# Cross-attention with an FP4 feed-forward: the group loop written out, the FP4 chain for h and the down product moved

## The reference

```python
x = x + tanh(g_xattn[0]) * xattn(layernorm(x), ctx, Wq, Wk, Wv, Wo, bo)
x = x + tanh(g_ffn[0]) * ffn(layernorm(x), w_gate, w_up, w_down)
# xattn: softmax(q k^T / 8) v per head, then @ Wo + bo
# ffn:   h = silu(fp4(x) @ fp4(w_gate).T) * (fp4(x) @ fp4(w_up).T); fp4(h) @ fp4(w_down).T
# fp4:   per 16 values: scale = max(|v|)/6; v/scale to the nearest of 0, .5, 1, 1.5, 2, 3, 4, 6; times scale
```

## Time and profile before

| | us |
|---|---|
| median of 3 runs | 598.71 (597.97 to 600.03) |
| the profiled execution | 598.33 |
| its span, first to last instruction | 596.1 |
| busy: PE, DVE, ACT, POOL | 543.8, 476.7, 312.3, 276.3 |

### The profile page before, as it was taken

One profiled execution on the slowest core, in us unless ns is written; L12 is line 12 of the kernel. 1 busy time (PEld: TensorE's weight loads), 2 busy tenths in 40 slices (PEclk: granted clock), 3 DMA queues, 4 the chain that ended last, 5 costly groups with the idle time before them and its releaser, 6 DMA issues.

```text
span 596.1 us, 9833 instructions
## 1 busy us (share of the span) xinstructions
PE 543.8 (91%) x2841; PEld 335.7 (56%) x2841; DVE 476.7 (80%) x793; ACT 312.3 (52%) x723; POOL 276.3 (46%) x234
## 2 busy tenths in 40 slices
PE   5889999999999998999999998999999999999642
PEld 4655565666566554666466554665566565656331
DVE  2769875889977996889977995789977997787655
ACT  3434756575456645575456644566456745546211
POOL 4007344553828173553828173363827264456400
PEclk9779999999999999999999999999999999999675
DMA  8500000200020000200020000200020000000000
GB/s 158 99 1 1 1 1 0 52 2 1 1 58 2 0 2 9 50 0 0 1 56 1 0 0 9 50 0 0 1 56 1 0 0 5 1 1 1 1 3 3
DMA packets 27892, 9.31 MB, mean 16 GB/s; under 512 B 24016, under 2 KB 27600, under 8 KB 27856
## 3 DMA queue, kind: packets, MB, share of 16 engines
q1 hardware_dynamic: 27856, 8.92, 7.5%
HBM read 8.50 MB, written 0.41 MB: 15 GB/s over the span
## 4 chain that ended last, share of the span: by engine, by line
PE 59%; DVE 27%; issue 10%; ACT 2%; DMA 1%; DVEq 0%; POOL 0%; SPq 0%; POOLq 0%; ACTq 0%
PE attn L789 16%; PE scores L775 11%; PE ring L728 10%; DVE max L897 8%; PE scores L776 7%; PE ring L735 4%; PE ring L742 4%; DVE f_abs L362 3%; DVE f_abs L364 2%; DVE e_gate L860 2%; DVE acc_v L919 2%; PE ring L707 2%; DVE h_fp L366 1%; DVE z L871 1%; DVE rsum L904 1%
## 5 line engine op out<-in xcount | busy, mean ns | idle before, releaser
L634 ACT ACTIVATE probs<-scores 120x400 f32<-120x400 f32 (+1 forms) x384 | 190.0, 504 | 211.7 <-PE scores L776 209.1
L897 DVE TENSOR_REDUCE max<-ring 116x1 f32<-116x482 f32 (+1 forms) x336 | 204.7, 649 | 28.4 <-PE ring L728 24.1
L505 POOL TENSOR_TENSOR acc_p<-acc_p,probs 120x800 f32<-120x800 f32 x79 | 156.3, 1978 | 61.7 <-ACT probs L634 58.1
L789 PE MATMUL attn<-probs,ctx_n 120*64 120x400 f32 (+1 forms) x768 | 173.9, 532 | 0.0
L775 PE MATMUL scores<-q_hh,k_hl 128*120 128x400 f32 (+1 forms) x384 | 155.0, 404 | 1.2 <-DVE q_ls L899 1.2
L775 PEld LDWEIGHTS scores<-q_hh,k_hl 128*120 128x120 f32 (+1 forms) x384 | 70.9, 185 | 128.2 <-ACT probs L634 70.2
L776 PE MATMUL scores<-q_ls,k_h 71*120 71x400 f32 (+1 forms) x384 | 134.8, 351 | 0.0
L728 PE MATMUL ring<-k_hl,q_hh 128*116 128x482 f32 (+1 forms) x336 | 119.6, 409 | 12.4 <-DVE max L897 4.7
L776 PEld LDWEIGHTS scores<-q_ls,k_h 71*120 71x120 f32 (+1 forms) x384 | 71.6, 186 | 4.2
L728 PEld LDWEIGHTS ring<-k_hl,q_hh 128*116 128x116 f32 (+1 forms) x336 | 59.1, 182 | 25.7 <-DVE max L897 9.9
L789 PEld LDWEIGHTS attn<-probs,ctx_n 120*64 120x64 f32 (+1 forms) x768 | 38.3, 136 | 46.4 <-issue 34.3
(11 more groups left out here) (127 smaller groups left out, 526.9 us busy)
## 6 DMA issues: line engine op xcount, KB each, us to landing
ctx_n<-in_ctx SPq DMA_DIRECT2D x16, 360.0 KB
wq<-in_L_xattn_Wq SPq DMA_DIRECT2D x1, 512.0 KB, 4.6
wo<-in_L_xattn_Wo SPq DMA_DIRECT2D x1, 512.0 KB, 6.8
x_in<-in_x SPq DMA_DIRECT2D x8, 50.0 KB
out<-y_out SPq DMA_DIRECT2D x8, 50.0 KB
wk<-in_L_xattn_Wk SPq DMA_DIRECT2D x1, 256.0 KB, 4.1
ctx_n<-in_ctx SPq DMA_DIRECT2D x16, 1.0 KB
wv<-in_L_xattn_Wv SPq DMA_DIRECT2D x1, 256.0 KB, 6.3
```

The source lines that it names most:

```text
L505: pool.tensor_tensor(acc_p[0:r, t.g % 2, :], left, probs[0:r, c % PROBS, :], ALU.add).then_inc(sum_p, 1)
L634: act.activation(probs[0:r, c % PROBS, k * HALF:(k + 1) * HALF], scores[0:r, slot % SCORE_BANKS, 0:HALF], ACT.Exp).then_inc(probs_full, 1)
L789: mm = pe.matmul(attn[64 * i:64 * i + C, k, 0:HALF], ctx_n[0:r, par, c, 0, :], probs[0:r, c % PROBS, k * HALF:(k + 1) * HALF], start=(j == ...
L897: dve.tensor_reduce(max3[0:rows, tile, part:part + 1], src[0:rows, 0:MAXC[part + 1] - MAXC[part]], AX.X, ALU.max).then_inc(free, 1)
```

## The change

The loop is gone: all 16 groups are written out on every engine, and the waits hold constants. In groups 3, 5, ..., 13 the nine links for h stand at slots 18 to 23, behind the maxima, and the transposes of h_fp4 and the down product stand in the even group after it, at slots 2, 3 and 5; its store follows there. Group 15 keeps the old slots (LAST_H_SLOTS, LAST_FFN_SLOTS), and the finish is as before.

```diff
-FFN_SLOTS = {2: ('zT', 0), 4: ('gate', 0), 6: ('up', 0), 19: ('hT', 0), 20: ('hT', 1), 22: ('down', 0)}
-W_SLOTS = {slot: ("wT", i) for i, slot in enumerate(FFN_SLOTS)}
+FFN_SLOTS = {2: ('zT', 0), 4: ('gate', 0), 6: ('up', 0)}
+DOWN_SLOTS = {2: ('hT', 0), 3: ('hT', 1), 5: ('down', 0)}
+LAST_FFN_SLOTS = {**FFN_SLOTS, 19: ('hT', 0), 20: ('hT', 1), 22: ('down', 0)}
+W_SLOTS = {slot: ("wT", i) for i, slot in enumerate(LAST_FFN_SLOTS)}
...
-H_SLOTS = [7, 8, 9, 10, 11, 12, 13, 14, 16]
+H_SLOTS = [18, 19, 19, 20, 21, 21, 22, 22, 23]
+LAST_H_SLOTS = [7, 8, 9, 10, 11, 12, 13, 14, 16]
...
-    if g % 2 and slot in FFN_SLOTS:
-        keys += [(FFN_SLOTS if g >= 3 else W_SLOTS)[slot]]
+    ffn = W_SLOTS if g == 1 else LAST_FFN_SLOTS if g == GROUPS - 1 else FFN_SLOTS if g % 2 else DOWN_SLOTS if g >= 4 else {}
+    if slot in ffn:
+        keys += [ffn[slot]]
...
+    def down_batch(self):
+
+        return self.batch(-1 if self.g % 2 or self.g == GROUPS else -2)
...
-            for g in (0, 1):
-                group(Turn(g))
-            with engine.Fori(0, (GROUPS - 4) // 4) as p:
-                for g in (2, 3, 4, 5):
-                    group(Turn(g, p))
-            for g in (GROUPS - 2, GROUPS - 1):
+            for g in range(GROUPS):
                 group(Turn(g))
             finish(Turn(GROUPS))
...
-                b, par = t.batch(-1), t.parity(-1)
+                b = t.down_batch()
+                par = b % 2
...
-                if t.g % 2 and t.g >= 3:
+                if t.g % 2 == 0 and t.g >= 4 or t.g == GROUPS - 1:
                     store(t)
...
-                    pe.wait_ge(hq4, LINKS * t.batch())
+                    pe.wait_ge(hq4, LINKS * (t.down_batch() + 1))
...
-                        if slot in H_SLOTS:
-                            h_fp4_link(t, H_SLOTS.index(slot))
+                        slots = LAST_H_SLOTS if t.g == GROUPS - 1 else H_SLOTS
+                        for link in [i for i in range(LINKS) if slots[i] == slot]:
+                            h_fp4_link(t, link)
```

More of the change, by code:

```diff
@@ L129, with __init__ @@
 RING = number_ring()
[L130 to L136, removed]
 class Turn:
-    def __init__(self, g, p=0):
-        self.g, self.p = g, p
+    def __init__(self, g):
+        self.g = g
     def count(self, per_group, plus):
-        return per_group * self.g + plus + (4 * per_group) * self.p
+        return per_group * self.g + plus
     def batch(self, ahead=0):
-        return self.g // 2 + ahead + 2 * self.p
+        return self.g // 2 + ahead
     def parity(self, ahead=0):
@@ L156, in fills @@
     def fills(self, ahead=0):
-        return (self.g // 2 + ahead) // 2 + 1 + self.p
+        return (self.g // 2 + ahead) // 2 + 1
     def ring(self, key):
         i = RING[(self.g, key)]
-        assert self.g >= 1 or isinstance(self.p, int)
-        return i % RING_BANKS, i // RING_BANKS + 1 + (RING_PER_LOOP // RING_BANKS) * self.p
+        return i % RING_BANKS, i // RING_BANKS + 1
+    def down_batch(self):
+        return self.batch(-1 if self.g % 2 or self.g == GROUPS else -2)
     def before(self):
-        return Turn(self.g - 1, self.p)
+        return Turn(self.g - 1)
 def xattn_ffn(nc, x, ctx_in, g_xattn, g_ffn, Wq, Wk, Wv, Wo, bo, w_gate, w_up, w_down, out):
@@ L905, in ring_use @@
                 elif kind == "down":
-                    par = t.parity(-1)
-                    dve.wait_ge(stored[par], 16 * t.fills(-1))
+                    par = t.down_batch() % 2
+                    dve.wait_ge(stored[par], 16 * (t.down_batch() // 2 + 1))
                     dve.scalar_tensor_tensor(out=y_out[0:N, par, :], in0=src[0:N, 0:D], scalar=tanh_f[0:N, :], in1=y[0:N, par, :],
@@ L999, in finish @@
             def finish(t):
-                add(Turn(t.g - 1, t.p), CHUNKS - 1)
+                add(t.before(), CHUNKS - 1)
                 add_last(t)
```

## The result

The changed kernel takes 588.16 us (587.77 to 588.68, 4 runs) against 598.34 us (597.93 to 600.03, 4 runs) for the kernel before on the same chip: ratio 0.9825, 95% interval 0.9804 to 0.9847. The forecast was 590.3 us, in a range of 585 to 597.

The account below looks back on a forecast made before the run. PE was taken as the engine to follow, losing time at two back edges and in odd groups waiting for h_fp4. 598.33 - 5.46 - 6.6 + 3.6 = 589.9 us profiled, 590.3 as a median; range 585 to 597.

Parts of the forecast that it names:

- The two back edges: Loop's branch, ahead of two even groups: writing the loop out removes both standstills and the lower clock, 5.46 us gained.
- rival (d): Loop written out: unrolling gives nothing because straight code is fetched as slowly as a branch's target, 595.8 us; chance 0.07.
- the register instructions: Loop body: the instructions that work out the waits vanish with the loop, neither a gain nor a loss.
- The six waits: PE, slot 19 of six odd groups: waits for h_fp4 of 1.1 us each go, 6.6 us gained.
- The chain at its new place: DVE, slots 18 to 23 of odd groups: nine links done 0.2 us before PE needs them, barely hidden.
- rival (c): DVE links 3 to 8, slots 20 to 23: GpSimd's additions keep the chain slow, 18 us lost, 604.6 us; chance 0.07.
- What is late next: Even groups: slot 4's maximum waits 0.5 us for a ring bank, 0.1 us remains at slot 2; six groups, +3.6 us.
- (a): Even groups after the move: clean, no new wait appears, 586.6 us; chance 0.22.
- (b): PE, slot 2 of even groups: the wait only moves, hT waits 1.1 us there, 596.8 us; chance 0.10.

Follow-up runs that it names:

- loop kept: Changed kernel with groups 4 to 11 as a loop of two passes, the other groups written out: 590.7 us, ratio 0.9876 to the kernel before.
- delayed run: Changed kernel with two more reductions of h on DVE between links 7 and 8 in groups 3 to 13: 590.0 us.
- busy GpSimd: Changed kernel with four more 120x800 additions on GpSimd behind its last one in groups 3 to 13: 636.0 us.
- gate at slot 5: Changed kernel, gate reciprocals at slots 9, 10, hT/down at 9, 12, 16 of even groups, odd groups' zT at 3, gate at 5: 578.1 us.

## Why the prediction was right, step by step

*The two back edges* (5.46 us): measured 5.4, as 1.9 us at group 6 and 3.5 at group 10, by the steps of slots 0 to 4 in the two traces. The straight code showed no standstill, so rival (d) falls. That the register instructions cost nothing holds for PE's steps from slot 8 to 18; but the loop's body and straight code differ by 0.06 us in the distance of GpSimd's additions, which the prediction had at nothing (loop kept).

*The six waits* (6.6 us): all gone. By the steps, 1.59 us less from slot 18 to 20, of which 0.36 is the transposes: 1.2 us each, 7.4 in all.

*The chain at its new place* was to be done 0.2 us before it is needed; it was 0.46 us. Link 3 began 0.1 us behind GpSimd's last addition, and the nine links took 3.77 us where 3.75 had been taken from the finish, a little under the 3.8 that was named as the least. The delayed run confirms that the reserve is small, and the busy GpSimd shows the mechanism of rival (c). It did not come about because GpSimd was done by 357.36, ahead of link 3 and 4.6 us ahead of the end of the chain.

*What is late next* (3.6 us) is the term that was mis-sized. The wait stands where it was put, at the maximum of slot 4, with 0.54 us idle on PE's loader. But the time from slot 0 to 4 grew by 0.64 us only, and 0.36 of that is the transposes: 0.3 us for each group, 1.7 in all, instead of 0.6 and 3.6. PE's loader had idled there before anyway, 0.32 and 0.30 us ahead of the two attn pairs and 0.23 for ScalarE ahead of the scores of slot 4; the first two are 0.23 now and the third is gone. PE's matmuls themselves stand still for 0.2 us:

```profile
365.25 0.47 PE L723 MATMUL ring<-k_hl,q_hh 128*116 128x480 f32 x1 [0.19 <-DVE max L892]
```

The sum of the prediction had given 0.3 us; it was raised to 0.5 because of the 0.68 us in the odd group, and that too is idle time of the loader. An idle interval is not a loss of the same length where the engine would have waited for another a moment later, and the loader's is not that of the matmuls.

*Not foreseen*: 0.12 us more from slot 2 to 4 of the odd groups and 0.08 less from 6 to 8, in straight code with or without the moved chain. z takes 1.89 us there instead of 1.83, which accounts for a part.

The pair of groups gained 0.9 us by these, where the prediction had 0.5; over six pairs that is the 2 us between 590.3 and 588.2. Both terms were off in the same direction, so the forecast is not right by two errors that cancel. Rivals (a) and (b) bounded it from both sides: (a) had no new wait at all and was 1.6 us off, so its number is a little nearer than the forecast's (2.1 us off), but the wait is there, and the trace decides for the forecast's mechanism; (b) is excluded by hT without a wait. Of the chances, those for a faster kernel add up to 0.86, where the prediction says 0.84.

## What to carry to other kernels

Work that makes an engine late is paid for at the first instruction that another engine needs from it, and it is worth moving only together with that instruction: in the written-out kernel, moving the reader alone led from 592.1 to 610.7 us, and moving both to 588.2. When two engines share a way into memory, place the short instructions of the one where the other's long ones have ended, and check the distance in the trace, since a start 0.06 us ahead of a long instruction or 0.14 us behind it decided over 1.6 us. Having unrolled and moved, look again: the two waits left over were worth as much as the change.

## What the hardware showed unexpectedly

- Single-input DVE instructions are held by GpSimd additions as two-input ones are: TENSOR_SCALAR of 100x352 took 1.92 and 2.02 us beside them, 0.34 alone; of 100x22, 1.79 against 0.18. Where DVE's addition of 120x800 ran beside them, it kept its 0.98 us, and GpSimd's took 2.96 us instead of 1.89.
- Waits of 1.5 us on PE were followed by some 6 us at the lower clock; waits of 1.1 us were not. Of the two back edges of the kernel before, about 2 us each, one was followed by it and one was not. Once it fell for some 3 us although PE had not stood idle in the 20 us before (gate at slot 5).
- A taken back edge costs 1.9 us on ScalarE, DVE and PE together, and 3.5 and 4.5 us in the two places where the lower clock followed.
- GpSimd's additions of 120x800 start 1.97 us apart in the loop's body and 2.03 us apart in straight code.
